# Attention with folded heads: values computed straight from 64-key blocks, second item of a pair shifted into the next step

## The chip, the cores and the metric

The kernel runs on one core of one Trainium2 chip. The metric is device time in microseconds of one execution, lower is better. Engines are named as in the profile: PE (TensorE matmul), PEld (its weight load), DVE (VectorE), ACT (ScalarE), POOL (GpSimd), SP (the queue that issues most DMAs).

## The reference, cut to what matters

Per batch item `x` is 128 tokens of 128 features (B = 32), the context is 77 keys of 128 features. All is float32.

```python
# self-attention, one head over 128 features
Q = x @ Wq.T + bq;  K = x @ Wk.T + bk;  V = x @ Wv.T + bv
x = layernorm(x + softmax(Q @ K.T / 8) @ V @ Wo.T + bo)
# cross-attention, H = 16 heads of 64 over the 77 context keys
q = x @ W_Q[h];  k = ctx @ W_K[h];  v = ctx @ W_V[h]
x = layernorm(x + concat_h(softmax(q @ k.T / 8) @ v) @ W_O)
# 8 experts; each takes the 1024 tokens (of 4096) with its highest gate
G, idx = top_k(softmax(x @ Wr).T, 1024)
x = layernorm(x + scatter_add(G * (gelu(x[idx] @ W1[e] + b1[e]) @ W2[e] + b2[e])))
```

## The kernel before, in words

**Folded weights.** Two set-up products per head are made once: M[h] = W_Q[h] W_K[h]^T / 8 and N[h] = W_V[h] W_O[h]. With them cross-attention needs two context products per head: A[h] = M[h] ctx^T, so that the scores are x1 A[h], and the folded values ctx N[h], so that the output is the sum over heads of probabilities times folded values. Both are made in three float32r products each (high and low halves of weights and context: hi*hi, hi*lo, lo*hi), for four batch items at once: 128 stationary features, 4 x 77 = 308 moving columns. The folded values come out transposed (`VOT`, features on the partitions), and ten 128x128 transposes per batch item turn them into `VO`, which has head-and-key rows on the partitions (16 x 77 = 1232 rows, ten chunks of 128, the last one padded).

**Steps.** Attention goes by pairs of batch items (16 pairs). Step p does cross-attention of pair p ("cross"), self-attention of pair p + 1 ("prep"), and the end of pair p - 1 ("post": its transposed rows and router logits). Steps -2 to 16 exist; the first and last are partial. Steps 1 to 12 are a loop of two steps per turn. In each even step, up to step 12, the values of four items (two pairs) are made (16 "VOT" units); in each odd step the A of four items (16 "A" units). The order inside a step is written out by hand for each engine, and each engine works its list strictly in order: `step` in the TensorE block (L1220), in the ScalarE block (L675), in the VectorE block (L873), in the GpSimd block (L568), in the SP block (L475).

**Hand-over.** TensorE's products go to a ring of four PSUM banks. `UNITS` (L39) lists what uses the ring, in order, and unit k takes bank k mod 4; TensorE waits until the copy of the unit four before has freed the bank. The scores of cross-attention have three banks of their own (`cross_scores`, L1242), and self-attention has one (`small`). Cross-attention of item e (0 or 1): scores, row maxima (L884), subtraction (L889), exp (ACT, L693), row sums (L895), reciprocal (L898), the product with it (POOL, L577), ten transposes (`cross_pT`, L1249), their copies, twenty product records against VO (`cross_out`, L1258), sum with x1 and statistics (L906 to L913), the power -1/2 on POOL (L588), and the normalised rows x2 (L878). Both items of the pair go through all of this in one step. VectorE copies heads 8 to 11 of each set of sixteen (`BY_DVE`), ScalarE the others.

**Self-attention.** Queries and keys are copied with their biases (L731, L733). The row maximum of the scores (L971) times -1/8 (L974) is the bias of the exp, whose scale is 1/8 (L712). The residual `r1` is written to SBUF (L923), its statistics follow (L929 to L936), then the power (POOL, L584) and x1 (L989), which TensorE transposes (L1392) and ScalarE copies (L780). The next step's first scores wait for that copy.

**Start and end.** GpSimd builds constants first, among them a chain of 31 selects (L557). Step -2 makes the values of pairs 0 and 1, then the M half of the set-up. In step 15 nothing is left to overlap, and TensorE runs filler products (`keep_warm`, L1180) between its pieces. Behind the attention stand the top-k by bisection, the gathers, the experts, the scatters and the last layer norm.

## Time and profile before

| | us |
|---|---|
| median of 3 runs | 668.06 (668.0 to 670.12) |
| the profiled execution, its own time | 665.35 |
| its span, first to last instruction | 663.4 |
| PE busy / PEld busy | 555.7 / 464.2 |
| DVE busy / ACT busy / POOL busy | 430.6 / 317.1 / 275.6 |
| mean granted TensorE clock | 0.92 of full speed |

A matmul's busy time includes the pipeline's length, so two neighbours overlap in it. What a product costs in a dense stretch is the distance from its start to the next one's start. In the rows, "x20" is a number of records; a plain float32 product is two records, a float32r product and a transpose are one each.

### The profile page before, as it was taken

To read this page: it belongs to the slowest core of one execution; us is meant where nothing else is said; L and a number is where in the kernel's file an instruction comes from. 1 tells how busy PE (TensorE), PEld (TensorE's weight loads), DVE (VectorE), ACT (ScalarE), POOL (GpSimd) and SP (SyncE) were. 2 spreads that over 40 slices of the span, in tenths; PEclk is the share of its full clock that TensorE was granted. 3 is DMA by queue.
4 is the path that set the end of the run, shared out by engine and by line. 5 is a ranking of instruction groups with operands and counts; after the bars stand their busy time and mean duration, and the time that the engine had idled before them with its cause. 6 is when DMAs were issued, how large, how long until landed. Compare 5 with 4: busy or idle time off the path is not lost.

```text
span 663.4 us, 11726 instructions
## 1 busy us (share of the span) xinstructions
PE 555.7 (84%) x3846; PEld 464.2 (70%) x3846; DVE 430.6 (65%) x1007; ACT 317.1 (48%) x721; POOL 275.6 (42%) x313
## 2 busy tenths in 40 slices
PE   9989999999999999999999979501399999897700
PEld 9868989989988988988988868301277775465600
DVE  3256766766775785685676667588855687424576
ACT  3655855765765675675676632100133334332215
POOL 7203233322322322332232233000677777777756
PEclk9999999999999999999999989655599999979765
DMA  5011220320221122023042100670123355534662
GB/s 187 27 41 39 97 76 14 96 87 10 86 87 51 45 87 89 8 87 96 0 150 72 55 17 9 227 170 0 42 57 109 125 181 176 171 109 142 217 230 111
DMA packets 50547, 61.09 MB, mean 92 GB/s; under 512 B 10578, under 2 KB 36435, under 8 KB 50260
## 3 DMA queue, kind: packets, MB, share of 16 engines
q1 hardware_dynamic: 45984, 52.00, 24.3%
q0 software_dynamic: 4096, 8.66, 4.6%
q8 instruction: 18, 0.29, 0.2%
q14 instruction: 13, 0.11, 0.1%
q10 hardware_dynamic: 436, 0.03, 0.0%
HBM read 35.37 MB, written 25.30 MB: 91 GB/s over the span
## 4 chain that ended last, share of the span: by engine, by line
PE 46%; DVE 25%; issue 12%; POOL 7%; ACT 6%; DMA 3%; DVEq 0%; POOLq 0%; ACTq 0%
PE PS L1238 10%; PE PS L1477 7%; PE PS L1459 7%; PE PS L1264 6%; PE PS L1246 6%; DVE csum L895 3%; POOL spread L612 3%; DVE above L1013 3%; DVE pc L889 3%; PE PS L1255 2%; DVE cmax L884 2%; POOL shared L602 2%; ACT VOeven L673 2%; DMA shared<-table,idx 2%; DVE shared L945 2%
## 5 line engine op out<-in xcount | busy, mean ns | idle before, releaser
L577 POOL TENSOR_TENSOR pn<-pc,crcp 128x1232 f32<-128x1232 f32 x32 | 72.0, 2250 | 180.2 <-DVE crcp L898 180.2
L602 POOL DMA_INDIRECT shared<-table,idx x64 | 63.1, 986 | 66.2 <-DVE idx L1077 47.3
L1238 PE MATMUL PS<-cT_hi,heads_hi 128*128 128x308 f32 x256 | 83.7, 327 | 1.1 <-DVE shared L945 0.6
L673 ACT ACTIVATE shared<-PS 128x308 f32<-128x308 f32 (+1 forms) x144 | 62.1, 472 | 42.2 <-PE PS L1273 29.8
L1238 PE MATMUL PS<-cT_hi,heads_lo 128*128 128x308 f32 x256 | 78.0, 305 | 0.0
L1238 PE MATMUL PS<-cT_lo,heads_hi 128*128 128x308 f32 x256 | 77.5, 303 | 0.0
L1246 PE MATMUL PS<-shared,x1T 128*128 128x512 f32 (+1 forms) x192 | 72.4, 513 | 4.4 <-DVE pc L889 4.0
L612 POOL DMA_INDIRECT spread<-pn,idx x64 | 66.2, 1034 | 19.8 <-issue 17.7
L808 ACT ACTIVATE shared<-PS,b1T 128x512 f32<-128x512 f32 x64 | 44.0, 687 | 56.0 <-PE PS L1459 56.0
L895 DVE TENSOR_REDUCE csum<-pc 128x16 f32<-128x1232 f32 x32 | 45.8, 1430 | 33.6 <-ACT pc L693 33.6
L1477 PEld LDWEIGHTS PS<-w,shared 128*128 128x128 f32 x512 | 63.8, 204 | 4.1 <-issue 3.8
L1477 PE MATMUL PS<-w,shared 128*128 128x128 f32 x512 | 65.0, 288 | 0.1
L1459 PE MATMUL PS<-pT,w 128*128 128x512 f32 x128 | 63.0, 627 | 0.8 <-ACT pT L797 0.7
L673 ACT ACTIVATE pT<-PS 128x512 f32<-128x512 f32 (+1 forms) x96 | 43.5, 527 | 38.5 <-PE PS L1255 38.2
L1246 PEld LDWEIGHTS PS<-shared,x1T 128*128 128x128 f32 x192 | 34.0, 190 | 37.1 <-issue 30.6
L588 POOL TENSOR_TENSOR rs<-ve,mhalf 128x1 f32<-128x1 f32 x32 | 17.3, 541 | 85.9 <-DVE ve L913 85.9
L1238 PEld LDWEIGHTS PS<-cT_hi,heads_hi 128*128 128x128 f32 x256 | 48.4, 189 | 3.3 <-DVE VOT L945 0.8
L673 ACT ACTIVATE VOT<-PS 128x308 f32<-128x308 f32 x96 | 40.2, 435 | 22.0 <-PE PS L1238 22.0
L797 ACT ACTIVATE pT<-PS 128x512 f32<-128x512 f32 x16 | 9.1, 595 | 85.4 <-PE PS L1450 85.4
L1238 PEld LDWEIGHTS PS<-cT_lo,heads_hi 128*128 128x128 f32 x256 | 48.5, 189 | 0.0
L1238 PEld LDWEIGHTS PS<-cT_hi,heads_lo 128*128 128x128 f32 x256 | 48.1, 188 | 0.0
L884 DVE TENSOR_REDUCE cmax<-PS 128x16 f32<-128x1232 f32 x32 | 44.9, 1403 | 3.4 <-PE PS L1246 3.3
(173 smaller groups left out, 1129.1 us busy)
## 6 DMA issues: line engine op xcount, KB each, us to landing
spread<-zeros SPq DMA_DIRECT2D x128, 128.0 KB, 2.1
VOT<-spread SPq DMA_DIRECT2D x64, 256.0 KB, 5.6
xboth<-in_x SPq DMA_DIRECT2D x16, 256.0 KB, 2.7
w<-in_W SPq DMA_DIRECT2D x2, 2048.0 KB, 11.0
table<-x SPq DMA_DIRECT2D x16, 128.0 KB, 1.9
fin<-table SPq DMA_DIRECT2D x1, 2048.0 KB, 20.4
out_x<-fin SPq DMA_DIRECT2D x8, 256.0 KB, 2.0
cin<-in_ctx SPq DMA_DIRECT2D x8, 154.0 KB, 2.6
```

Source lines behind the costliest of these rows:

```text
L577: pool.tensor_tensor(pn[:, e, 0:HK].rearrange("p (h k) -> p h k", h=HEADS), pc[:, e, :].rearrange("p (h k) -> p h k", h=HEADS), crcp[:, e, ...
L602: pool.indirect_dma_start(xg[:, e % 3, h, :], None, table, bass.IndirectOffsetOnAxis(ap=idx[:, e, h:h + 1], axis=0)).then_inc(gathered[e % ...
L612: pool.indirect_dma_start(spread[e], bass.IndirectOffsetOnAxis(ap=idx[:, e, h:h + 1], axis=0), ye[:, e % 2, h, :], None).then_inc(scattere ...
L673: act.activation(dst, src, ACT.Copy).then_inc(free[bank_of(at, name)], 1)
L808: act.activation(hid[:, c, 512 * h:512 * h + 512], PS[:, HID_BANKS[(2 * FC * e + n) % len(HID_BANKS)], :], ACT.Gelu, bias=b1T[:, FC * e + ...
L884: dve.tensor_reduce(cmax[:, e, :], s, AX.X, ALU.max).then_inc(cmax_done, 1)
L895: dve.tensor_reduce(csum[:, e, :], pc[:, e, :].rearrange("p (h k) -> p h k", h=HEADS), AX.X, ALU.add).then_inc(csum_done, 1)
L1238: i = pe.matmul(bank[:, 0:4 * KEYS], w[a][:, h, :], cT[b][:, :], start=(n == 0), stop=(n == 2))
L1246: i = pe.matmul(PS[:, n, 0:b - a], x1T[:, e, :], A[:, 2 * parity + e, a:b], start=True, stop=True)
L1264: i = pe.matmul(bank[:, 0:P], pT[:, e, c * P:(c + 1) * P], VO[parity][:, e, c, :], start=(c == 0), stop=(c == CH - 1))
L1459: pe.matmul(PS[:, HID_BANKS[k % len(HID_BANKS)], :], w1[:, e, c * P:(c + 1) * P], xeT[:, 512 * h:512 * h + 512], start=True, stop=True).th ...
L1477: i = pe.matmul(y_bank(e, h, s), hid[:, c, (4 * h + s) * P:(4 * h + s + 1) * P], w2[:, e, c, :], start=(c == 0), stop=(c == FC - 1))
```

## The change

- The folded values are computed with the keys as the stationary operand, so they come out with keys on the partitions and need no transpose. 64 of the 77 keys of both items of a pair make one stationary block of 128; it is multiplied with four heads at once (512 moving columns). A pair takes four such units ("VO" units, `values`), each of three float32r products. Each unit is copied in two halves of 64 partitions; VectorE copies one unit of the four, ScalarE three.
- The other 13 keys of eight items (104 rows) make a second stationary block: four "rest" units per four pairs, copied to a staging tile, stored to DRAM by 8 DMAs per half and loaded by 2 DMAs per pair into chunks 8 and 9 of VO.
- The normalised probabilities are written on POOL in two instructions, 64 keys and 13 keys of each head, to match the order of rows.
- A is made for eight heads in every step instead of sixteen in every odd one; it is held for three pairs.
- The transposes and the output product of a pair's item 1, with statistics and norm, move to the next step.
- The queries are scaled by -1/8 when they are copied, the row minimum of the scores is the bias of the exp, the multiplication L974 goes, and r1 stays in PSUM.
- The loop has four steps per turn. POOL also copies the high and low halves of the 64 keys (`main_keys`). Step -2 makes the values of pair 0 and the four rest units of the first four pairs. The tile for the returned expert rows moves from VOT to the end of the tile of A.

```diff
-UNITS = [ ... VOT_UNITS ... A_UNITS ... P2T_UNITS ... ]      # two lists, even and odd
+def units_of(phase):
+    units = [(("P2T", 1, g), "post") for g in range(3)]
+    units += [("QK", "prep"), ("V", "prep"), (("AV2", 1), "post")]
+    units += [(("VO", u), "values") for u in range(2)]
+    if phase == 3:
+        units += [(("A", h), "A first") for h in range(8)]
+    heads = [(("A", h), "A even" if phase % 2 == 0 else "A odd") for h in early_heads(phase)]
+    units += heads[0:3] + [(("P2T", 0, g), "cross") for g in range(3)] + [("x2T", "post")]
+    units += heads[3:6] + [(("AV2", 0), "cross")]
+    if phase in (1, 2):
+        units += [(("rest", u), "rest 1" if phase == 1 else "rest 2") for u in range(2 * phase - 2, 2 * phase)]
+    units += heads[6:8] + [(("VO", u), "values") for u in range(2, 4)] + [("LG", "post")]
+    if phase == 2:
+        units += [(("rest", u), "rest first") for u in range(2)]
```

The GpSimd step:

```diff
-                            pn[:, e, 0:HK]..., pc[:, e, :]..., crcp..., ALU.mult).then_inc(pn_done, 1)
+                def main_keys():
+                    if parity == 0:
+                        wait_apart(pool, ct_lo, nth + 2, passed_pool)
+                    for k in range(2):
+                        i = pool.tensor_copy(cmain[k][:, parity, :]..., cT[k]...[:, 2 * parity:2 * parity + 2, 0:KEYS_MAIN])
+                    i.then_inc(cmain_done, 1)
+                def divided(e):
+                    wait(pool, crcp_done, 2 * p + e + 1)
+                    for at_pn, a, b in ((0, 0, KEYS_MAIN), (HEADS * KEYS_MAIN, KEYS_MAIN, KEYS)):
+                        i = pool.tensor_tensor(pn..., pc...[:, :, a:b], crcp..., ALU.mult)
+                    i.then_inc(pn_done, 1)
+                # order: xbo, divided(0), power of item 1 of p - 1, main_keys, power of LN1, divided(1), power of item 0
```

The TensorE step, in its new order (function names as before; `values`, `rest_values` are new):

```diff
+                def values(u):
+                    hi, lo = [t[:, values_pair(at), :] for t in cmain]
+                    h = 8 * (u % 2) + u // 2
+                    n_hi, n_lo = [t[:, h:h + 7:2, :] for t in NN]
+                    done(products(unit(("VO", u)), ((hi, n_hi), (lo, n_hi), (hi, n_lo))), ("VO", u))
-                vo_transposes(...)                  # 20 per pair
                 cross_scores(0)
+                cross_pT(p - 1, 1)                  # if post; 10 filler products first in step 16
                 QK, V
+                cross_out(1, 1 - parity)
                 self_scores()
+                values(0); values(1)                # waits for cmain_done
                 cross_scores(1)
+                heads(mine[0:3])                    # in step -1: heads(range(8)) too, around the self-attention
                 self_transposes()
                 cross_pT(p, 0)
                 x2T
                 self_values()
+                heads(mine[3:6])
                 cross_out(0, parity)
+                rest_values(...)                    # two units in phases 1 and 2, steps 1, 2, 5, 6, 9, 10
+                heads(mine[6:8])
+                values(2)
                 x1T
+                values(3)
                 router()
```

The VectorE step: maximum, subtraction and sum of item 0; cT_lo (even steps), crest_lo; the minimum L971; statistics of (p - 1, item 1); two half copies of VO unit 1; maximum of item 1; norm of (p - 1, item 1); subtraction of item 1; first_norm; sum of item 1; x1; statistics and norm of (p, item 0). In step -1 it copies heads 2, 3, 6, 7 before first_norm and 10, 11, 14, 15 after x1.

```diff
-                                                     r1[:, e, :] (SBUF) in L923, L929, L989; L974 snb = smax * -SELF_SCALE
+                        r1 = small[:, e * P:(e + 1) * P]
+                        i = dve.scalar_tensor_tensor(out=r1, in0=r1, scalar=srcp[:, e:e + 1], in1=xbo[:, e, :], ...)
+                        i = dve.bn_stats(st1[:, e, :], small[:, e * P:(e + 1) * P])
```

The SP step adds `load_rest_keys` (once per turn), `load_rest` (2 DMAs, waiting for the output product of item 1 of the pair before) and `store_rest` (8 DMAs, after two rest units are copied).

## Rows read from the trace of the kernel before

**Rows 1.** Busy time by stage: us, PE, PEld, DVE, ACT, POOL, clock, DMA share, GB/s.
```profile
0.00:41.47 41.47, 37.35 (x288) 35.19 (x288) 14.11 (x45) 22.72 (x53) 18.78 (x63) 1.00 0.25 86
41.47:64.75 23.28, 22.00 (x150) 19.44 (x151) 15.36 (x30) 13.68 (x33) 5.76 (x4) 1.00 0.17 57
64.75:374.86 310.11, 306.08 (x2171) 274.44 (x2169) 213.86 (x448) 198.33 (x490) 92.65 (x91) 1.00 0.21 66
374.86:397.05 22.19, 17.75 (x111) 14.88 (x109) 14.98 (x30) 9.41 (x22) 7.12 (x7) 0.92 0.16 53
397.05:420.20 23.15, 19.21 (x140) 16.20 (x138) 15.29 (x26) 5.91 (x11) 6.12 (x5) 1.00 0.02 6
420.20:663.40 243.20, 153.29 (x994) 104.05 (x994) 157.00 (x429) 67.02 (x112) 145.22 (x143) 0.79 0.45 141
```

**Rows 2.** Who waited for whom, 60 to 400 us: total, times, longest.
```profile
PE PS L1246 <- DVE pc L889: 3.4, 7, 0.5
```

**Rows 3.** Timeline of TensorE: start, us, engine, line, operation, records, idle before.
```profile
160.02 2.23 PE L1246 MATMUL PS<-shared,x1T 128*128 128x512 f32 x6
162.09 1.03 PE L1319 MATMUL PS<-xboth,wT 128*128 128x256 f32 x4
163.40 0.38 PE L1332 MATMUL PS<-ident,x 128*128 128x128 f32 x2
...
192.51 0.30 PE L1238 MATMUL PS<-cT_lo,heads_hi 128*128 128x308 f32 x1
...
196.87 0.31 PE L1238 MATMUL PS<-cT_hi,heads_lo 128*128 128x308 f32 x1
...
201.01 2.39 PE L1264 MATMUL PS<-VOeven,pT 128*128 128x128 f32 x20
203.24 1.25 PE L1255 MATMUL PS<-ident,pn 128*128 128x128 f32 x10
204.33 0.51 PE L1281 MATMUL PS<-wr,x2T 128*128 128x8 f32 x4
```

**Rows 4.** All instructions by line and shape: busy us, mean ns, idle before.
```profile
L838 DVE SCALAR_TENSOR_TENSOR heads_lo<-PS,heads_hi 128x512 fp32r<-128x512 f32 x8 | 5.0, 683 | 8.4 <-ACT heads_hi L661 8.4
L577 POOL TENSOR_TENSOR pn<-pc,crcp 128x1232 f32<-128x1232 f32 x32 | 72.0, 2250 | 180.2 <-DVE crcp L898 180.2
L945 DVE COPY VOT<-PS 128x308 f32<-128x308 f32 x32 | 13.4, 469 | 6.6 <-PE PS L1238 6.6
L961 DVE TENSOR_TENSOR cT_lo<-cin,cT_hi 128x308 fp32r<-128x308 f32 x8 | 3.8, 469 | 0.0
```

**Rows 5.** Timeline of VectorE in step 5, columns as in rows 3.
```profile
162.41 1.43 DVE L884 TENSOR_REDUCE cmax<-PS 128x16 f32<-128x1232 f32 x1
163.87 1.44 DVE L889 TENSOR_TENSOR pc<-PS,cmax 128x1232 f32<-128x1232 f32 x1
...
175.07 1.42 DVE L895 TENSOR_REDUCE csum<-pc 128x16 f32<-128x1232 f32 x1
...
176.69 0.11 DVE L918 RECIPROCAL srcp<-ssum 128x2 f32<-128x2 f32 x1
...
179.95 0.60 DVE L989 TENSOR_SCALAR x<-r,mv,rs 128x128 f32<-128x128 f32 x2 [0.82 <-POOL rs L584]
...
182.25 0.34 DVE L878 TENSOR_SCALAR x<-r,mv,rs 128x128 f32<-128x128 f32 x1 [0.65 <-POOL rs L588]
```

**Rows 6.** Timeline of ScalarE in the same step: the copies of one item's probabilities.
```profile
175.04 1.35 ACT L673 ACTIVATE pT<-PS 128x512 f32<-128x512 f32 x3
```

**Rows 7.** Timeline of TensorE in the first 60 us.
```profile
13.66 0.39 PE L1238 MATMUL PS<-cT_hi,heads_hi 128*128 128x308 f32 x1
```

**Rows 8.** Timeline of POOL at the start: the last of its constants.
```profile
21.64 0.29 POOL L565 CAST before<-beforef 128x128 bf16<-128x128 f32 x1
```

**Rows 9.** Busy time by stage around an idle stretch of TensorE, columns as in rows 1.
```profile
382.00:387.00 5.00, 1.29 (x9) 1.10 (x8) 4.93 (x6) 0.81 (x4) 2.25 (x1) 0.96 0.08 28
387.00:390.00 3.00, 3.00 (x16) 2.96 (x15) 1.67 (x4) 2.81 (x5) 0.00 (x0) 0.50 0.00 0
```

More of the change, by code:

```diff
@@ L49, with runs @@
     while len(units) % RING_BANKS:
         units.append((("none", len(units)), None))
+    return units
+def runs(stage, q):
+    if stage == "prep":
+        return -1 <= q < PAIRS - 1
+    if stage == "cross":
+        return 0 <= q < PAIRS
+    if stage == "post":
+        return 1 <= q <= PAIRS
+    if stage == "ahead":
+        return q % 2 == 0 and -2 <= q < PAIRS - 2
+    if stage == "main keys":
+        return -2 <= q < PAIRS - 2
+    if stage == "A first":
+        return q == -1
+    if stage == "A even":
+        return q % 2 == 0 and 0 <= q < PAIRS - 2
+    if stage == "A odd":
+        return q % 2 == 1 and -1 <= q < PAIRS - 2
+    if stage == "values":
+        return q == -2 or 0 <= q < PAIRS - 1
+    if stage == "rest first":
+        return q == -2
+    if stage == "rest 1":
+        return q % PHASES == 1 and 1 <= q < PAIRS - 4
+    if stage == "rest 2":
+        return q % PHASES == 2 and -2 <= q < PAIRS - 4
+    return False
@@ new lines, in step @@
+                if values:
+                    values_copy(0)
+                    values_copy(1)
+                if prep:
+                    self_exp()
+                if first == -1:
+                    self_pT()
+                    heads_copy(range(8))
+                if heads:
+                    heads_copy(mine[0:3])
+                if prep and cross:
+                    self_pT()
+                if cross:
+                    if first == 0:
+                        act.wait_ge(rest_out, 16 * 4 * PHASES)
+                    cross_pT(0)
@@ L957, in step @@
                     cross_sub(0)
-                if even:
+                    cross_sum(0)
+                if runs("ahead", first):
                     wait(dve, ct_hi, nth + 2)
@@ L1347, in step @@
-                if even:
-                    wait(pe, ct_lo, nth + 2)
-                if isinstance(p, int) and p == -2:
-                    for k in range(FIRST):
-                        setup_wait_copied(pe, k)
-                if isinstance(p, int) and p == -1:
-                    for k in range(FIRST, len(SETUP)):
-                        setup_wait_copied(pe, k)
-                if products:
-                    heads(0, 4)
-                if first:
-                    self_values()
@@ L1389, in step @@
+                if runs("rest 1", first):
+                    wait(pe, cr_lo, turn + 2)
+                    rest_values(0)
+                    rest_values(1)
+                if runs("rest 2", first):
+                    if first == -2:
+                        pe.wait_ge(cr_lo, 1)
+                    rest_values(2)
+                    rest_values(3)
+                if ahead:
+                    heads(mine[6:8])
+                if runs("values", first):
+                    values(2)
                 if prep:
@@ L1393, in step @@
                     i.then_inc(self_full, 1)
-                if cross:
-                    cross_out(1)
+                if runs("values", first):
+                    values(3)
+                if post:
+                    router()
+                if runs("rest first", first):
+                    rest_values(0)
+                    rest_values(1)
+                if first == -2:
+                    for k in range(FIRST, len(SETUP)):
+                        set_up_unit(k)
+                    pe.wait_ge(route_in, 16 * 3)
             attention_steps(pe, step)
             for k in range(RING_BANKS):
-                n = sum(active(q, stage) for q in range(-2, PAIRS + 1) for j, (_, stage) in enumerate(UNITS[q % 2])
+                n = sum(runs(stage, q) for q in range(-2, PAIRS + 1) for j, (_, stage) in enumerate(UNITS[q % PHASES])
                         if j % RING_BANKS == k)
```

600 lines of the change are left out of this document (340 added, 260 removed).

## The prediction

> **What bounds the kernel now.** I read the busy shares by stage first [rows 1]. Steps 1 to 13 of the attention last 310.11 us, 23.85 us a step; TensorE is busy in 306.08 of them at full clock, VectorE in 213.86, ScalarE in 198.33. The start takes 41.47 us, step 0 23.28, step 14 22.19, and step 15 up to the last x2 23.15. The last 243.2 us are top-k and experts, which the change leaves alone. Then the waits: the largest of TensorE's own inside the steps is 3.4 us in 7 waits [rows 2]. So it is TensorE's list of work that sets the length of a step. Overlapping busy times don't price it, so I take distances between starts [rows 3]: three float32 score products (6 records, 1232 columns) 162.09 - 160.02 = 2.07 us; QK and V 1.31; a float32r product of 308 columns (196.87 - 192.51) / 31 = 0.141; an output product (20 records) 2.23, so 4 records are 0.45; ten transposes 1.09; the router 0.4 (its four records show 0.51).
>
> **TensorE's work in a step, before and after.** Both: scores 2 x 2.07, probability transposes 2 x 1.09, outputs 2 x 2.23, QK and V 1.31, self scores and values 2 x 0.45, three double transposes 3 x 0.22, router 0.37: 14.0 us. Before there are also 24 products of 308 columns on average for A and 24 for the values, 48 x 0.141 = 6.77, and 20 value transposes, 2.18: 22.97 us, against 23.85 measured, so 0.9 a step are stalls and refills. After: 24 products for A, 3.38; 12 products of 512 columns. The trace has no float32r product that wide. Bounds: 512 columns in proportion to 0.141 are 0.234; 0.141 plus the additional 204 columns at the rate of the score products (two records per column, 2.07 / 2464 = 0.84 ns a record column, a half of it if float32r goes once) is 0.227; nothing above 308 columns free of charge is the floor, 0.141. I take 0.22, near the upper two: 2.64. Sum 20.05 us. In six of the thirteen steps (1, 2, 5, 6, 9, 10) two rest units add 6 x 0.22 = 1.32. Thirteen steps: 13 x 20.05 + 7.9 = 268.6 us without a stall, 280 if the old 0.9 stays in each.
>
> **Does another engine bind then?** Time from the start of a step's first scores; VectorE's list with distances of [rows 5]. Maximum of item 0 at 2.4, subtraction 3.85 to 5.3. ScalarE has by then copied the three groups of the older item's probabilities (1.35 each time [rows 6]) and QKV, and the exp runs 5.35 to 6.6. Sum and reciprocal (1.62) to 8.3. Minimum 0.4; statistics of the older item 1.1 (179.95 + 0.6 to 182.25 - 0.65) to 9.8; the two half copies to 11.0; maximum 12.4; norm 12.7; subtraction 14.0; first_norm 2.3 to 16.3; sum 18.0; x1 18.6. TensorE comes to x1's transposes at 18.8, so it is just not kept waiting. They, VO unit 3 and the router end at 20.05, and the next scores start. The probabilities of item 0 leave POOL at 10.9, TensorE wants them at 12.0; the older item's rows x2 are ready at 12.7, wanted at 13.1; bank 2 (output of item 0, freed by VectorE behind x1 at 18.8) is wanted at 19.0. In even steps cT_lo pushes VectorE's list by 0.35 and TensorE waits some 0.2. Everything fits, with 0.2 to 1 us of room: I put 0.4 a step on it, 5.2 in all. So 273.8 against 310.1: **-36.3**.
>
> **Single edits.** Half copies: the nearest row is a 512-column pass from PSUM, 0.683 [rows 4]; two are 1.25, below nothing is excluded as the four head copies (4 x 0.4) that they replace are gone; cover VectorE's list above. If 64 partitions cost double, the list grows by 1.2. POOL's product in two instructions: 2.25 for one now; two cost between 2.25 and 4.5; I take 2.5, since 1232 elements are the same and one more start is added. Cover: 1.1 us before TensorE wants them; behind it on POOL stand the power that the norm at 12.3 waits for, so the upper end would cost 1.2 on VectorE's list. L974's removal saves 0.4 of VectorE's list, counted. Negated scaling rides on a copy that exists: nothing. ScalarE: eight head copies, six half copies, a rest copy per two steps in place of twelve heads and six VO copies: about 17 us of 20.5, no bound. POOL's main_keys: two copies of 128 elements, under 1 us between item 0's product (10.9) and LN1's power (16.3). SP: load_rest waits for an output product done at 6.7, then 8 clears, then the store of x2; store_rest last; the loaded rows are wanted 28 us after their issue. Nothing on the path; if SP were late it would show at `cross_out(0)`.
>
> r1 in PSUM: two statistics passes and two scalings now read PSUM. The row of a copy from PSUM, 308 elements in 469 ns, is as long as an SBUF-only subtraction of the same size, 469 [rows 4]; so I charge nothing for it. The Trainium skill (VectorE: DVE Perf Modes, "The TRN2 errata" and "Why PSUM operands drop a tier") puts 62 cycles more on a PSUM source and takes the doubled rate from a float32 scaling. By that rule the four instructions would add an estimated 0.4 us to VectorE's list and use up the room; the pair of rows speaks against the fixed part of it.
>
> **Start: a loss.** The first value products ran at 13.66 [rows 7]. Now they wait for POOL's main_keys, and POOL is in its chain of constants until 21.93 [rows 8]; two memsets less (0.35), two copies more: 22.3. TensorE then has 8 units of 3 x 0.22, 5.3 us. It has idled 8 us, though, and rows show what follows: after 5 us with 1.29 of busy time, 387 to 390 ran at clock 0.50, which is 1.2 GHz, and the next stretch was back near full [rows 9]. That costs 1.7. Fold and M set-up 3.7 us as before: step -1 starts at 33, 8 us later than before. In step -1 the value transposes go (3.3 us), but heads 14 and 15 wait for VectorE's copies of 10 and 11, which stand behind x1: about 14.6 us instead of 16.4. First scores at 47.5: **+6.1**. **Step 0** has no older item: VectorE's list is shorter by the statistics and norm, and x1 ends it: 18.6 against 23.3, **-4.7**. **Step 14** has no heads; VectorE's list holds it at 19.9 against 22.2: **-2.3**.
>
> **End: a loss.** In step 15 the older item's transposes and output stand in front of the filler and the second scores, which start at 9.4 instead of 5.7. The rest of the chain follows: maximum 11.8, subtraction 15.0, exp 16.5, sum 18.2, POOL's product 20.7, transposes 22.3, copies 23.3, output 25.6, statistics, power and norm 2.3: 27.9 against 23.1: **+4.8**. The tail behind is unchanged.
>
> Sum: -36.3 + 6.1 - 4.7 - 2.3 + 4.8 = -32.4. The profiled execution took 665.35 (span 663.4 and 1.95 around it), 2.7 below the median of the runs; 668.06 - 32.4 = 635.7, **636 us**.
>
> **Rivals.**
> 1. *VectorE's list becomes the bound.* For: it has 0.2 us of room, and four of its neighbours are priced from rows of other shapes. Against: its sum of work is 16 us. With POOL's pair at its upper end (+1.2) and 0.5 for reads of PSUM and half copies, x1 ends at 20.3 and a step lasts 21.6, with a rest unit 22.3. 7 x 21.6 + 6 x 22.3 = 285, 11 more than forecast, and steps 0 and 14 1.7 each: 650 us.
> 2. *Slower: wide float32r products run at half rate.* Mechanism: a product of 512 columns takes 0.43 us, as a record of the float32 scores does (2.07 / 2464 x 512). Place: all 16 x 12 value and 48 rest products, 240 x 0.21 = 50 us: 686 us. It turns the sign from 0.355 us per product. Against: the 308-column products go once, at 0.141.
> 3. *The stalls stay.* What kept TensorE waiting 0.9 us a step before was the order of hand-overs; if it stays, 280 instead of 273.8: 642 us.
>
> **How the numbers follow.** Forecast 0.45, stalls stay 0.25, VectorE's list 0.22, half rate 0.05, and 0.03 for a change that moves nothing because gains are eaten. The range goes from the stall-free sum with 0.21 per product and a start 2 us shorter (628) to the second case with 2 us more (652). Within 0.3% is what a measurement here can't tell from no change. Faster 0.92 (the first three), same 0.03, slower 0.05.
>
> **What would show it.** Right: first scores near 47 us with TensorE idle from 14 to 22; distances of 20.1 to 21.5 us between steps; products of 512 columns 0.22 us apart; step 15 some 5 us longer. Wrong: TensorE waiting for x1 (L989) or x2 in every step (rival 1); products 0.4 apart (rival 2); waits for `rest_in` ahead of the outputs, which I charged nothing.

## The result, and the profile after

| | before | changed |
|---|---|---|
| median of the runs, us | 668.03 (666.09 to 670.12, 4 runs) | 635.27 (634.73 to 635.82, 4 runs) |
| ratio | | 0.951, 95% interval 0.948 to 0.954 |
| profiled execution, its time and its span | 665.35, 663.4 | 635.82, 633.9 |
| PE busy / PEld busy | 555.7 / 464.2 | 524.8 / 423.6 |
| DVE / ACT / POOL busy | 430.6 / 317.1 / 275.6 | 415.4 / 316.8 / 289.0 |

The median is 32.8 us lower and lies where it was forecast. The profiled executions differ by 29.5 us only, because that of before was 2.7 below its median and that of the changed kernel 0.5 above its own. The forecast of -32.4 was made between profiled executions, so measured like for like it is 3 us too large.

The busy shares by stage of the changed kernel, cut where the first cross scores of steps 0, 1, 14 and 15 and the last norm begin; the last cut of [rows 1] lies 0.4 us later, where that norm ends (start:end, length, busy us and count of PE, PEld, DVE, ACT and POOL, then granted clock, DMA share, GB/s):

```profile
0.00:50.76 50.76, 36.34 (x234) 31.80 (x234) 15.45 (x47) 18.63 (x40) 19.38 (x65) 0.89 0.31 92
50.76:70.80 20.04, 18.60 (x98) 14.25 (x99) 13.97 (x26) 10.71 (x26) 5.64 (x7) 0.93 0.24 79
70.80:342.96 272.16, 271.89 (x1779) 235.52 (x1779) 198.66 (x413) 199.12 (x450) 104.31 (x146) 1.00 0.31 92
342.96:362.20 19.24, 17.64 (x112) 14.13 (x112) 14.78 (x31) 11.86 (x26) 6.01 (x7) 1.00 0.39 128
362.20:390.20 28.00, 24.43 (x190) 21.80 (x189) 14.81 (x26) 9.38 (x19) 7.65 (x10) 1.00 0.02 6
390.20:633.90 243.70, 155.92 (x994) 106.13 (x994) 157.71 (x430) 67.16 (x112) 146.01 (x143) 0.78 0.45 141
```

The third line holds the gain: thirteen steps in 272.16 us instead of 310.11, with TensorE busy in all but 0.27 us. Seven steps without rest units last 20.3 us (one 20.8), six with them 21.6. The first line holds a loss: the first scores begin at 50.76 instead of 41.47. That start shows in TensorE's timeline (start, length, engine, line, operation, count, and in brackets the idle time before and what ended it):

```profile
22.22 0.77 PE L1408 MATMUL PS<-heads_hi,cmain_hi 128*128 128x512 f32 x1 [7.57 <-POOL cmain_lo L700]
...
26.70 0.73 PE L1408 MATMUL PS<-heads_hi,crest_hi 128*104 128x512 f32 x1 [1.57 <-DVE VOeven L1117]
...
29.35 0.62 PE L1408 MATMUL PS<-heads_hi,cmain_hi 128*128 128x512 f32 x1
29.78 0.42 PE L1408 MATMUL PS<-heads_hi,cmain_lo 128*128 128x512 f32 x1
30.04 0.40 PE L1408 MATMUL PS<-heads_lo,cmain_hi 128*128 128x512 f32 x1
...
48.96 0.41 PE L1408 MATMUL PS<-cT_hi,heads_hi 128*128 128x308 f32 x1 [1.65 <-DVE shared L1106]
...
50.76 3.79 PE L1438 MATMUL PS<-shared,x1T 128*128 128x512 f32 x6 [0.47 <-ACT x1T L857]
```

After 7.57 us without work TensorE runs at the lower of its two clocks, 1.2 GHz (granted clock 0.50): the value products are 0.43 us apart until 29.78, then 0.26, and 0.23 after that. From 29.78 to 49 the granted clock is 1.00. Then it falls a second time: the first scores take 3.79 us where those of the next steps take 2.3, at 0.50.

In a full step, the product of 512 columns shows its price in the same view:

```profile
142.28 0.40 PE L1408 MATMUL PS<-heads_hi,cmain_hi 128*128 128x512 f32 x1
142.51 0.39 PE L1408 MATMUL PS<-heads_hi,cmain_lo 128*128 128x512 f32 x1
142.74 0.39 PE L1408 MATMUL PS<-heads_lo,cmain_hi 128*128 128x512 f32 x1
142.97 1.45 PE L1438 MATMUL PS<-shared,x1T 128*128 128x512 f32 x3
```

From 142.28 to 142.97 are three products, 0.23 us each. VectorE's and POOL's timelines of the step that begins at 134.35, around the parts that changed:

```profile
144.30 1.39 DVE L1117 COPY shared<-PS 64x512 f32<-64x512 f32 x2
145.72 1.44 DVE L1050 TENSOR_REDUCE cmax<-PS 128x16 f32<-128x1232 f32 x1
...
149.61 0.49 DVE L1094 BATCH_NORM_STATS2 st<-PS 128x6 f32<-128x128 f32 x2
...
152.25 0.64 DVE L1166 TENSOR_SCALAR x<-PS,mv,rs 128x128 f32<-128x128 f32 x2
```

```profile
142.73 2.52 POOL L708 TENSOR_TENSOR pn<-pc,crcp 128x1024 f32<-128x1024 f32 x2 [7.22 <-DVE crcp L1064]
...
152.41 2.43 POOL L708 TENSOR_TENSOR pn<-pc,crcp 128x1024 f32<-128x1024 f32 x2 [0.92 <-DVE crcp L1064]
```

The first of these two fences holds three of the prediction's prices: two half copies 1.39 to 1.42 us (predicted 1.25), statistics from PSUM 0.49 for two, and x1 done at 152.25 + 0.64 = 152.9, which is 18.5 us after the scores (predicted 18.6). The last line of it and the last of POOL's overlap; that becomes important below.

### The profile page after: what moved, and what is told of

Same layout as the page of the kernel before. It is cut to its first block, busy times and chain, and to the rows that moved or that the text cites. A ratio compares the mean times of both kernels' runs of the same rounds, so it can differ in the third digit from the quotient of the medians.

```text
span 633.9 us, 10905 instructions
## 1 busy us (share of the span) xinstructions
PE 524.8 (83%) x3402; PEld 423.6 (67%) x3402; DVE 415.4 (66%) x971; ACT 316.8 (50%) x670; POOL 289.0 (46%) x375
## 4 chain that ended last, share of the span: by engine, by line
PE 68%; DVE 13%; POOL 9%; issue 4%; DMA 3%; ACT 2%; POOLq 0%; ACTq 0%; DVEq 0%
PE PS L1408 17%; PE PS L1438 11%; PE PS L1460 10%; PE PS L1655 7%; PE PS L1673 7%; PE PS L1448 5%; POOL spread L753 3%; DVE above L1188 3%; POOL shared L743 2%; PE PS L1510 2%; POOL groupf L674 2%; DMA shared<-table,idx 2%; DVE pc L1245 1%; PE PS L1476 1%; PE PS L1489 1%
## 5 line engine op out<-in xcount | busy, mean ns | idle before, releaser
L708 POOL TENSOR_TENSOR pn<-pc,crcp 128x1024 f32<-128x1024 f32 x64 | 78.6, 1248 | 146.6 <-DVE crcp L1064 146.6
L971 ACT ACTIVATE shared<-PS,b1T 128x512 f32<-128x512 f32 x64 | 44.0, 687 | 58.4 <-PE PS L1655 58.4
L814 ACT ACTIVATE shared<-PS 128x308 f32<-128x308 f32 x120 | 47.5, 434 | 30.3 <-PE PS L1408 30.2
L814 ACT ACTIVATE pT<-PS 128x512 f32<-128x512 f32 (+2 forms) x100 | 45.8, 528 | 22.5 <-PE PS L1448 18.4
L1055 DVE TENSOR_TENSOR pc<-PS,cmax 128x1232 f32<-128x1232 f32 x32 | 46.0, 1438 | 0.6
L726 POOL TENSOR_TENSOR rs<-ve,mhalf 128x2 f32<-128x2 f32 x16 | 11.2, 702 | 76.7 <-DVE ve L1101 76.7
L1655 PEld LDWEIGHTS PS<-pT,w 128*128 128x128 f32 x128 | 21.3, 196 | 36.0 <-ACT shared L971 23.9
L1408 PE MATMUL PS<-cT_hi,heads_hi 128*128 128x308 f32 x128 | 43.0, 336 | 2.3 <-DVE shared L1106 1.7
L826 ACT ACTIVATE pc<-pc 128x1232 f32<-128x1232 f32 x32 | 39.7, 1241 | 2.8 <-DVE pc L1055 2.8
L1448 PE MATMUL PS<-ident,pn 128*128 128x128 f32 (+1 forms) x320 | 40.2, 273 | 0.5 <-POOL pn L708 0.5
L842 ACT ACTIVATE VOeven<-PS 64x512 f32<-64x512 f32 x48 | 28.4, 592 | 24.1 <-PE PS L1408 23.4
```

The source lines that it names most:

```text
L708: i = pool.tensor_tensor(pn[:, e, at_pn:at_pn + HEADS * (b - a)].rearrange("p (h k) -> p h k", h=HEADS), pc[:, e, :].rearrange("p (h k) -> ...
L814: act.activation(dst, src, ACT.Copy).then_inc(free[bank_of(at, name)], 1)
L1055: dve.tensor_tensor(pc[:, e, :].rearrange("p (h k) -> p h k", h=HEADS), s, cmax[:, e, :].unsqueeze(2).to_broadcast([P, HEADS, KEYS]), ALU. ...
L1408: i = pe.matmul(bank, a, b, start=(n == 0), stop=(n == len(pairs) - 1))
L1448: i = pe.transpose(bank[0:rows, (c - a) * P:(c - a + 1) * P], pn[:, e, n:n + rows], ident[:, :])
L1655: pe.matmul(PS[:, HID_BANKS[k % len(HID_BANKS)], :], w1[:, e, c * P:(c + 1) * P], xeT[:, 512 * h:512 * h + 512], start=True, stop=True).th ...
```

## The experiments

Twelve kernels ran, in three sets of four. In the first and third set the kernel before had medians of 667.9 and 666.7 us. The second set ran on a chip on which it had 709.65. In its kernels the part behind the attention took some 285 us at clock 0.74 instead of 243 at 0.78, while steps 1 to 13, where an edit leaves them alone, took 272.16 and 272.15 us as in the changed kernel. Absolute times are therefore not compared across sets, only ratios and lengths of stages; the changed kernel itself was not run in the second and third set.

**The changed kernel again**, as the base of the first set.

> The changed kernel again, as the control of the kernels beside it. Same as its first timing: 635.3 us (634.7 to 635.8).

Measured: 634.92 us (632.74 to 635.76), ratio 0.950, interval 0.947 to 0.954; first scores 49.69, steps 1 to 13 in 272.17 us. The start varies between executions, the steps do not. Here the wait for the keys is as long, but TensorE was back at full clock after the gap in the middle of the value products, which are 0.23 to 0.29 us apart from this line on:

```profile
26.79 0.45 PE L1408 MATMUL PS<-heads_hi,crest_hi 128*104 128x512 f32 x1 [1.57 <-DVE VOeven L1117]
```

That alone makes the first scores 1.07 us earlier than in the first profile. The start's other part that varies is the second fall of the clock. Of the kernels below with this start and its waits, the one with the scalings ahead of the reciprocal has it at the first scores as well (3.79 us), the one without fillers in step 15 has it earlier, in the heads' products, and those with the small product alone and with two value units on VectorE have none (first scores in 2.34 us). Where it comes it costs 1.5 us. What decides it is open, so these 1.5 us are not put down to an edit.

### The start

**POOL makes the keys of step -2 in the middle of its constants.**

```diff
                 pool.wait_ge(consts, 18 + n + P // E)
+                if n == 0:
+                    pool.wait_ge(ct_lo, 1)
+                    for k in range(2):      # the two casts of main_keys()
+                        i = pool.tensor_copy(cmain[k][...], cT[k][...])
+                    i.then_inc(cmain_done, 1)
...
-                if runs("main keys", first):
+                if runs("main keys", first) and first != -2:
                     main_keys()
```

> POOL copies the 64 keys of step -2 after 16 of its 31 constant selects instead of behind all of them. Theory A (the wait at the start is the cause of the loss there, and the half clock follows from it): TensorE starts the value products at about 13.9 instead of 22.2 and at full clock, so 8.3 + 3.7 = 12 us come back; first scores at 39, 623.5 us. Theory B (something else at the start is late too, the weights of M or the copies of the rest units): less than half of it, 629 us or more.

Measured: 623.7 us (620.86 to 624.78), ratio 0.934, interval 0.932 to 0.937, against 0.950 in the same set. POOL's and TensorE's timelines of this kernel:

```profile
3.57 8.53 POOL L674 TENSOR_SCALAR_AFFINE_SELECT groupf<-groupf 128x128 f32<-128x128 f32 x16
12.17 0.29 POOL L680 CAST cmain_hi<-cT_hi 128x128 fp32r<-128x128 f32 x1
12.41 0.29 POOL L680 CAST cmain_lo<-cT_lo 128x128 fp32r<-128x128 f32 x1
12.65 7.98 POOL L674 TENSOR_SCALAR_AFFINE_SELECT groupf<-groupf 128x128 f32<-128x128 f32 x15
```

```profile
13.66 0.48 PE L1415 MATMUL PS<-heads_hi,cmain_hi 128*128 128x512 f32 x1
...
16.87 0.45 PE L1415 MATMUL PS<-heads_hi,crest_hi 128*104 128x512 f32 x1 [1.57 <-DVE VOeven L1124]
```

The value products start at 13.66, as they did before the change [rows 7], and at full clock. First scores are at 39.75, 9.9 us earlier than in the base of this set, and step 0 takes 18.58 us, the 18.6 that was predicted for it. Theory A holds: two casts of 0.29 us that stood at the end of a chain of constants cost 11.2 us (634.92 - 623.7). The traces divide it: 8.7 us of waiting (22.32 - 13.66), 1.3 in the value products at half clock, and 1.5 in step 0, where the clock did not fall (that part may not be the keys' doing, as said above).

**The wait kept, the clock held up.** 34 filler products ahead of the wait for the keys.

```diff
                 if runs("values", first):
+                    if first == -2:
+                        keep_warm(34, 6)
                     wait(pe, cmain_done, ...)
```

> The wait for POOL stays, but TensorE runs 34 filler matmuls in it (about 7.6 us), so it does not stand idle. Theory A (7.4 us of value products at half clock are the result of the idle stretch): the clock stays at full speed, the eight units take 5.5 us instead of 9.2, 631.5 to 632.5 us. Theory B (the clock plays no part, the copies of the units set their rate): no change, 635.3.

Measured: 632.4 us (630.84 to 633.96), ratio 0.946, interval 0.943 to 0.950, which overlaps the base's. The trace is clearer than the times: the eight units end at 29.92 instead of 31.43 in the base of this set, yet the first scores begin at 49.69 in both. Two stretches of this kernel and then the two of the base that answer to them (columns as in the stages above) show what took it back:

```profile
36.00:38.00 2.00, 0.55 (x5) 0.39 (x5) 0.42 (x1) 0.81 (x4) 0.00 (x0) 1.00 0.64 121
38.00:42.00 4.00, 4.00 (x19) 4.00 (x20) 0.96 (x2) 1.25 (x4) 0.00 (x0) 0.57 0.74 198
```

```profile
37.50:39.50 2.00, 0.55 (x5) 0.39 (x5) 0.42 (x1) 0.81 (x4) 0.00 (x0) 1.00 0.67 124
39.50:43.00 3.50, 3.50 (x26) 3.50 (x27) 1.06 (x3) 2.10 (x5) 0.00 (x0) 1.00 0.72 184
```

Here the clock fell behind the first exp of the self-attention, and the heads' products ran slower for 4 us; then step 0 takes 18.55 us instead of 20.08. The base lost the same 1.5 us at its first scores, so that fall only changed its place: step 1 begins at 68.24 instead of 69.77, and those 1.5 us are what the value products gained. Theory A holds for them. The medians differ by 2.5 (634.92 - 632.4), but their intervals overlap. The missing keys cost the larger part.

**Heads 10, 11, 14 and 15 of the first step copied by ScalarE.**

```diff
-            return at.first == -1 and h % 8 in FIRST_HEADS_BY_DVE
+            return at.first == -1 and h in FIRST_HEADS_BY_DVE
```

> In the first step that makes heads for a pair, four of the head banks (10, 11, 14 and 15) are copied out by ScalarE instead of VectorE. TensorE had waited 1.65 us for VectorE's copies of 10 and 11, which stand behind the first x1. Theory A (that wait sets the first cross scores at 50.76, and the half clock that follows it makes those scores 3.79 instead of 2.23 us): first scores 1.3 to 1.7 us earlier, step 0 up to 1.5 us shorter, 632 to 634 us. Theory B (ScalarE's copies delay x1's transposed copy, on which the same scores wait, by their own four times 0.6 us): first scores at the same place or up to 1 us later, 635 to 636 us.

Measured (second set): 676.41 us (675.27 to 678.4), ratio 0.954, interval 0.951 to 0.956. First scores 48.94, step 0 18.57: step 1 starts at 67.51, against 69.77 to 71.63 in the four kernels that have the changed kernel's start and step 0 (with r1 in SBUF in one of them). From the set-up's product L1373, where the value products are done, to the first scores are 16.57 us (32.37 to 48.94) instead of 18.26 in both executions of the changed kernel: the wait of 1.65 us is gone and nothing took its place. So the first half of theory A holds, with 1.7 us, and theory B falls. The second half, that the wait brings the half clock of the first scores, isn't shown: three kernels with the wait have those scores at full clock too. The ratio of the whole doesn't show the gain.

### The shift of the half pair

**Item 1's transposes, output, statistics and norm back in their own step**, the keys stationary and the self-attention as changed.

```diff
-    units = [(("P2T", 1, g), "post") for g in range(3)]
-    units += [("QK", "prep"), ("V", "prep"), (("AV2", 1), "post")]
+    units = [("QK", "prep"), ("V", "prep")]
...
-    units += heads[6:8] + [(("VO", u), "values") for u in range(2, 4)] + [("LG", "post")]
+    units += heads[6:8] + [(("P2T", 1, g), "cross") for g in range(3)]
+    units += [(("VO", u), "values") for u in range(2, 4)] + [(("AV2", 1), "cross"), ("LG", "post")]
```

with the engines' lists moved in the same way.

> Item 1's transposes, output, statistics stay in their own step, as before; everything else of the change is kept. Theory A (without the shift the chain through VectorE and POOL to item 1's product, ready 19.4 us into the step, is the bound and the output product has to follow it): a step lasts about 24.7 us, 13 x 24.7 = 321 instead of 272, step 0 four more, step 15 five less: 683 us. Theory B (TensorE's list is the bound either way and the shift is worth only the stalls of 0.9 us a step that the kernel before had): 647 us.

Measured: 696.98 us (696.39 to 699.29), ratio 1.043, interval 1.040 to 1.046: slower than the kernel before. Step 1 begins at 76.08 and step 14 at 398.09, 24.8 us a step against 20.9, with TensorE busy in 286.84 of 322.01 us. TensorE's largest group of waits in this kernel from 76 to 400 us (waiting and waited for, us in total, times, longest), and one case of it in its timeline:

```profile
PE PS L1447 <- POOL pn L709: 25.8, 26, 2.0
```

```profile
168.90 1.62 PE L1447 MATMUL PS<-ident,pn 128*128 128x128 f32 x10 [1.96 <-POOL pn L709]
171.59 0.63 PE L1575 MATMUL PS<-ident,x 128*128 128x128 f32 x2
```

The shorter list of TensorE is worth nothing in this order without the shift: TensorE has run out of other work before item 1's probabilities leave POOL, it waits for them in 26 places, and the transposes that follow at 171.59 take 0.63 us instead of 0.44. The chain of theory A holds, and its 24.7 us a step. The shift removes no instruction, and yet the keys' 2.9 us less of TensorE's work a step (22.97 to 20.05 in the prediction's sum) count only with it. Two things stay open: the kernel before had no shift either and took 23.85 us a step, and what makes this one 0.9 longer was not isolated; and the shift with the old values was not run.

### The self-attention's part

**The whole part undone**: queries unscaled, the maximum times -1/8 on VectorE, r1 in SBUF.

```diff
-                                      ALU.min).then_inc(smin_done, 1)
+                                      ALU.max).then_inc(smin_done, 1)
+                    dve.tensor_scalar(snb[:, :], smin[:, :], -SELF_SCALE, None, ALU.mult).then_inc(snb_done, 1)
...
-                        i = dve.scalar_tensor_tensor(out=r1, in0=r1,
+                        i = dve.scalar_tensor_tensor(out=r1s[:, e, :], in0=r1,
```

> The self-attention part of the change undone, everything else kept: the queries unscaled, the scale again in the exponential with an extra small VectorE product on the maxima, and the residual written to SBUF instead of back into PSUM. It adds one VectorE instruction of about 0.1 us and its wait to each step. Theory A (TensorE's list sets the step, with 271.89 of 272.16 us busy in steps 1 to 13, and what PSUM costs VectorE against SBUF is nothing, as the statistics took 0.49 us for two from either): the step keeps its length, the whole is 0 to +2 us on the changed kernel's 635 us. Theory B (the small product with its hop to ScalarE delays the exponential, and with it the probabilities and x1, by 0.3 to 0.5 us a step that TensorE then waits): +4 to +7 us over 15 steps.

Measured (second set): 722.47 us (720.4 to 723.91), ratio 1.018, interval 1.015 to 1.020. Both theories fail. Steps 1 to 13 take 307.87 us (75.70 to 383.57) instead of 272.16: 2.75 a step, and the whole gain of the change is gone with an edit that the prediction priced at 0.4 us of VectorE's list for the product and at nothing for r1. Two groups of VectorE's instructions in this kernel, from 95 to 300 us (line, operation, shapes, count, busy, mean ns of one, idle before):

```profile
L1171 DVE TENSOR_SCALAR x<-r,mv,rs 128x128 f32<-128x128 f32 x18 | 19.5, 1125 | 0.0
L1143 DVE TENSOR_SCALAR snb<-smin 128x2 f32<-128x2 f32 x9 | 13.6, 1516 | 0.3
```

A product of two elements per partition takes 1516 ns. The next three kernels ask why.

**r1 in SBUF alone.** Of the diff above the last two lines, and the statistics and the scaling reading `r1s`.

> The changed kernel with the self-attention's residual in SBUF alone undone; the scaling stays in the queries. With the whole self-attention part undone a step took 22.85 us instead of 20.27, and two rows had grown: the two scalings to x1 took 2.17 us together instead of 0.64, and the small product on the maxima 1.71 us. Both stood beside POOL's pair of products on the probabilities. Theory A (a VectorE scaling whose operands are all in SBUF is held up until a running POOL product ends; from PSUM it is not): the two scalings take 1.5 to 2.2 us, a step 1.1 to 1.5 us longer, 21.4 to 21.8 us without rest units, and the whole 15 to 20 us more than the changed kernel's. Theory B (the scalings were late only because the small product was): the scalings take 0.6 to 0.7 us and the step stays at 20.3.

Measured: 656.63 us (652.42 to 658.32), ratio 0.983, interval 0.978 to 0.987. Steps 1 to 13 take 287.14 us, 1.15 a step more. VectorE's and POOL's timelines of this kernel:

```profile
158.31 0.25 DVE L1065 RECIPROCAL crcp<-csum 128x16 f32<-128x16 f32 x1
158.48 2.16 DVE L1167 TENSOR_SCALAR x<-r,mv,rs 128x128 f32<-128x128 f32 x2
```

```profile
158.64 2.42 POOL L709 TENSOR_TENSOR pn<-pc,crcp 128x1024 f32<-128x1024 f32 x2 [0.92 <-DVE crcp L1065]
```

**The small product alone.** Of the diff above the first three lines, r1 in PSUM.

> The changed kernel with the scaling back in the exponential, which needs the small product of 128x2 elements on VectorE again; the residual stays in PSUM. Theory A (as for the residual: all its operands are in SBUF and it starts just behind the start of POOL's product of item 0, so it lasts until the first of POOL's two instructions or both have ended): the product takes 1.4 to 1.7 us instead of the 0.1 to 0.2 that two elements need, a step 1.0 to 1.5 us longer, the whole 13 to 20 us more. Together with the residual's 1.1 to 1.5 that makes the 2.6 us of the whole part. Theory B (the product's own length is 0.2 us and the hand-over to ScalarE costs 0.3): a step is 0 to 0.3 us longer.

Measured: 654.72 us (652.27 to 656.01), ratio 0.982, interval 0.979 to 0.985. Steps 1 to 13 take 289.86 us, 1.36 a step more. The same two views of this kernel:

```profile
145.91 1.43 DVE L1142 TENSOR_SCALAR snb<-smin 128x2 f32<-128x2 f32 x1
...
156.27 0.64 DVE L1170 TENSOR_SCALAR x<-PS,mv,rs 128x128 f32<-128x128 f32 x2
```

```profile
145.29 2.53 POOL L710 TENSOR_TENSOR pn<-pc,crcp 128x1024 f32<-128x1024 f32 x2 [6.74 <-DVE crcp L1066]
...
156.43 2.43 POOL L710 TENSOR_TENSOR pn<-pc,crcp 128x1024 f32<-128x1024 f32 x2 [0.92 <-DVE crcp L1066]
```

POOL's record holds two instructions: the first takes 2.02 us at 145.29 and 1.92 at 158.64, the second 0.55. The small product ends at 147.34, when the first of them does (145.29 + 2.02 = 147.31). At 38.3, in step -1, where POOL stands still from 34.5 to 45.6, the same instruction of this kernel takes 0.17 us. The scalings with r1 in SBUF end at 160.64, again with the first (158.64 + 1.92 = 160.56); of the two, one takes 0.25 us and the other 2.0. With r1 in PSUM the same scalings beside the same product take 0.64 us together.

**r1 in SBUF, but the scalings ahead of the reciprocal** that lets POOL's product start.

```diff
                     dve.tensor_reduce(csum[:, e, :], ...).then_inc(csum_done, 1)
+
+                def cross_rcp(e):      # cross_rcp(0) stays behind the sum of item 0
                     wait(dve, csum_done, 2 * p + e + 1)
                     dve.reciprocal(crcp[:, e, :], csum[:, e, :]).then_inc(crcp_done, 1)
...
                         dve.tensor_scalar(x1[1 - parity][:, e, :], r1s[:, e, :], ...)
                 if cross:
+                    cross_rcp(1)
                     second_stats(p, 0, parity)
```

> The residual in SBUF as before the change (scaling still in the queries), and on VectorE the two scalings to x1 moved ahead of the reciprocal of item 1's sum, so that POOL's product of item 1, which waits for that reciprocal, cannot have started. Same instructions, same operands, another order of two. Theory A (the scalings are held up by POOL's running product): they take 0.6 to 0.7 us again, x1 is as early as in the changed kernel or 0.2 us earlier, the step is back at 20.3 us (21.6 with rest units), and the whole within 0.5% of the changed kernel. Theory B (operands in SBUF are slow by themselves, or another engine's traffic slows them): 1.1 us each as with the whole part undone, a step of 21.4 us or more.

Measured: 635.5 us (633.89 to 636.85), ratio 0.953, interval 0.949 to 0.956, that of the changed kernel; steps 1 to 13 take 271.91 us (changed 272.16). VectorE and POOL:

```profile
152.43 0.59 DVE L1170 TENSOR_SCALAR x<-r,mv,rs 128x128 f32<-128x128 f32 x2
152.94 0.24 DVE L1067 RECIPROCAL crcp<-csum 128x16 f32<-128x16 f32 x1
```

```profile
153.26 2.43 POOL L709 TENSOR_TENSOR pn<-pc,crcp 128x1024 f32<-128x1024 f32 x2 [1.30 <-DVE crcp L1067]
```

Same instructions and operands, other order, 21 us less than with r1 in SBUF and the order as it was, 15.2 of them in steps 1 to 13. Theory A holds. So it is neither SBUF as such nor the scaling: a VectorE scaling from SBUF to SBUF that meets a running POOL product waits until that ends. The Trainium skill states this (SBUF — State Buffer, "Who interferes with whom"): VectorE's two-port modes and GpSimd share one pair of ports, and the one that comes second "fully blocks". This case's traces agree, with 1.43 to 2.16 us, and a source in PSUM kept VectorE out of it.

### The room on VectorE, and the end

**VectorE copies two value units of four.**

```diff
-VALUES_BY_DVE = (1,)
+VALUES_BY_DVE = (0, 1)
```

> VectorE also copies the first of the four value units of a step, which ScalarE copied: about 1.4 us more on VectorE's list in each of 16 steps and about 1.2 us less on ScalarE's. This measures the room on VectorE's list beside TensorE's. Theory A (VectorE's list from the scores to the x1 that the next scores need has less than 0.5 us of room, as the walk of the changed kernel has it: x1 ends 18.5 us after the scores in a step of 20.3): the added copy delays x1 and the step grows by 0.9 to 1.1 us, 647 to 651 us on the whole, with TensorE idle that much in each step. Theory B (VectorE's idle time of some 5 us a step takes the copy up, since the copy stands before a wait for TensorE): the step grows by under 0.2 us, the whole by under 3 us.

Measured (second set): 694.85 us (691.4 to 697.73), ratio 0.979, interval 0.975 to 0.982. Steps 1 to 13 take 287.84 us, 1.21 more a step for 1.4 added. That is theory A, a little above its 0.9 to 1.1: VectorE's list has about 0.2 us of room (1.4 less 1.21) beside TensorE's.

**No fillers ahead of step 15's second scores and of step 16's transposes.**

```diff
-                    keep_warm(10 if first == PAIRS else 0)
+                    keep_warm(0)
...
-                    keep_warm(14 if alone else 0)
+                    keep_warm(0)
```

> Leaves out the 14 filler products ahead of step 15's second half pair's scores and the 10 ahead of the transposes after it, which the changed kernel has because steps 15 and 16 have no next pair to prepare. Theory A (they stand in front of work that is ready before they end, so the path shortens by what they cover): the second scores began at 371.93 behind fillers that ran to about 371.9, and the last stretch from 362.20 to 390.20 gets 1 to 3 us shorter, 632 to 634 us on the whole. Theory B (the fillers keep the granted clock at full speed; without them it falls to half, and the scores, transposes and outputs of the end, some 3.4 us of work at full clock, take twice that): 0 to +3 us, with half clock in the slices from 368 to 390.

Measured (second set): 678.43 us (674.18 to 680.66), ratio 0.954, interval 0.951 to 0.958. The second scores come 6.60 us after the first instead of 9.73, but from step 15's first scores to the last norm are 27.28 us instead of 27.92. TensorE in this kernel:

```profile
369.62 2.23 PE L1438 MATMUL PS<-shared,x1T 128*128 128x512 f32 x6
...
381.77 1.31 PE L1448 MATMUL PS<-ident,pn 128*128 128x128 f32 x10 [1.56 <-POOL pn L708]
383.97 4.61 PE L1460 MATMUL PS<-shared,pT 128*128 128x128 f32 x20 [0.89 <-ACT pT L814]
```

Both theories are half right. The 14 fillers stood in the way; the 10 kept the clock up (without them 0.50 was granted from 384 to 389). Without them the last output product takes 4.61 us instead of 2.47 and hands back most of the gain.

**Together**: the early keys, the heads by ScalarE, the 14 fillers out, the 10 kept.

> Three edits on the changed kernel that gained alone, together: POOL makes the keys of step -2 in the middle of its chain of constants, ScalarE instead of VectorE copies heads 10, 11, 14 and 15 of the first step, and the 14 fillers ahead of step 15's second scores are gone, while the 10 ahead of the transposes of step 16 stay, since without them the granted clock fell to half at 384 and the last output product took 4.61 instead of 2.47 us. Theory A (they add up, as each lies on another stretch of the path): first scores 39.7 less 0.5 to 1.5 us, step 15 to the last x2 26.0 instead of 28.0, together -13 to -15 us on the changed kernel, a ratio to the kernel before of 0.928 to 0.933 where the changed kernel had 0.951. Theory B (the heads' copies gained only because TensorE's clock was down at the start, which the earlier keys already mend): -12.5 to -13.5, ratio 0.931 to 0.935.

Measured: 619.11 us (618.8 to 620.96), ratio 0.928, interval 0.926 to 0.931, the fastest kernel here, and within theory A's ratio. Step 15 to the last norm takes 25.68 us, 2.2 less. But the first scores are at 40.70, 0.95 later than with the early keys alone, as ScalarE's timeline shows:

```profile
36.82 3.38 ACT L821 ACTIVATE shared<-PS 128x308 f32<-128x308 f32 x8 [1.29 <-PE PS L1415]
40.26 0.38 ACT L864 ACTIVATE x1T<-PS 128x256 f32<-128x256 f32 x1
```

x1's transposed copy stands behind eight head copies; with VectorE copying four of the heads it began at 39.32. So the heads' edit should be left out once the keys are early; that combination wasn't run. In the traces this kernel reaches the last norm 1.3 us before the one with early keys alone (376.33 and 377.61), and the two profiled executions are equally long (620.96 and 620.86); the rest of the difference between their ratios, 0.928 and 0.934, is seen in no stage of the attention.

## Why the prediction was right, and where not

Term by term, in us between the same marks (the last norm ends at 420.16 before and at 390.46 after):

| | predicted | measured |
|---|---|---|
| first scores later | +6.1 | +9.3 |
| step 0 | -4.7 | -3.2 |
| steps 1 to 13 | -36.3 | -38.0 |
| step 14 | -2.3 | -3.0 |
| step 15 to the end of the last norm | +4.8 | +5.1 |
| the rest | 0 | +0.2 |
| span | -32.4 | -29.5 |

- **The bound was read rightly.** TensorE's list set the step [rows 1 to 3], and the sum of that list priced it: 20.05 us without a stall against 20.27 measured. The 0.4 us a step put on for stalls was too much. The wide products, the one unknown with far ends, cost 0.23, near the two upper bounds, so rival 2 falls. The pair of POOL's products cost 2.43 to 2.52 us, predicted 2.5.
- **"The stalls stay" falls.** The 0.9 us a step of before went with the shift. Without the shift a step is 4 us longer than with it; the prediction had no term for that.
- **Rival 1 was nearer than its 0.22 says.** The changed kernel has 0.2 us of room on VectorE, and it has them because r1 lies in PSUM and the small product is gone.
- **"r1 in PSUM ... I charge nothing for it"** is right for what it asked, two statistics at 0.49 us, as from SBUF before (the row at 177.57 below), and two scalings at 0.64 against 0.60 [rows 5]. The four instructions cost 0.04 us more than from SBUF, not the 0.4 of the prediction's other estimate. It asked the wrong question. It compared the instruction by itself, not beside the neighbour that it gets in the new order, where the edit saves 1.15 us a step.
- **"L974's removal saves 0.4"** was too small for the same reason: in the new order it would cost 1.5 us on VectorE's list and 1.36 a step. The trace of before had the clue. There, VectorE and POOL show:

```profile
171.56 0.70 DVE L974 TENSOR_SCALAR snb<-smax 128x2 f32<-128x2 f32 x1
...
177.57 0.49 DVE L929 BATCH_NORM_STATS2 st<-r 128x6 f32<-128x128 f32 x2
...
178.49 0.64 DVE L936 TENSOR_SCALAR ve<-mv 128x2 f32<-128x2 f32 x1
```

```profile
169.98 2.25 POOL L577 TENSOR_TENSOR pn<-pc,crcp 128x1232 f32<-128x1232 f32 x1 [7.17 <-DVE crcp L898]
176.86 2.25 POOL L577 TENSOR_TENSOR pn<-pc,crcp 128x1232 f32<-128x1232 f32 x1 [4.62 <-DVE crcp L898]
```

The two small products, the first and the last of VectorE's rows, end with POOL's product: 172.26 and 172.23, 179.13 and 179.11. Their lengths were taken for their own. In step -1 of the same trace, at 28.4, where POOL stood still, L974 took 0.17 us instead of 0.70.
- **The start: the mechanism was right, the size off.** 22.3 was predicted for the first value product and 22.22 came; 3.7 for fold and set-up and 3.70 came; 14.6 for step -1 and 14.56 came. The miss of 3.2 us lies in the eight value units. "8 units of 3 x 0.22, 5.3 us" is the term that failed most: at full clock, in the kernel with early keys, they take 7.85 us (13.66 to 21.51), because TensorE waits 1.57 us for VectorE's copy of a value unit and shorter times for others, which the prediction didn't have. "That costs 1.7", for the half clock, came out at 2.4 here (10.28 us from 22.22 to 32.50) and at 1.3 in the changed kernel's second execution, so its size was about right. The 1.4 us by which step 0 missed are the second fall of the clock, which the prediction didn't have; where its first scores run at full clock, step 0 takes the predicted 18.6 (18.58 with early keys, 18.58 without the fillers of step 15).
- **The end** was walked wait by wait and came out at 5.1 us, predicted 4.8.
- **The range's lower end** doesn't add up: 635.7 less 5.2 for the stalls, 2.4 for 0.01 us on 240 products and 2 for the start is 626, where 628 stands. Nothing hangs on it.

That the median was met owes something to the two profiled executions lying on different sides of their medians; steps 1 to 14 came out 2.3 us better and the start with step 0 4.7 us worse, so part of the agreement is errors that cancel.

## What to carry to other kernels

Price an instruction beside the neighbour that it will have on the other engines, not from its mean. A tiny VectorE instruction of over half a microsecond that ends when a POOL instruction ends, as in the four cases here, is waiting for it; the same line at a place where POOL stands still gives its own length. Give it a PSUM operand, or move it ahead of what starts POOL. When an engine's list gets shorter, ask whether its inputs come early enough to use it; and look for the new first input of an engine at the end of another engine's set-up.

## What the runs showed of the hardware that was not expected

- A VectorE scaling of 128x2 elements from SBUF to SBUF took 1516 ns on average beside a POOL product of some 2.0 us, and 168 ns where POOL stood still; one of 128x128 up to 2.0 us instead of 0.3 (two in 0.59). The same scaling with its source in PSUM took 361 ns beside the same POOL product. VectorE's copies from PSUM at 144.30, beside POOL's product from 142.73 to 145.25, kept their length.
- A float32r product of 512 columns costs 0.229 us, one of 308 columns 0.141: 0.43 ns for each further column. At half clock the former costs 0.43 us.
- After 7.57 us of idling TensorE's clock stayed at the lower level for 7.6 us of work with one gap of 1.57 us in it. After 8.12 us of idling, in the changed kernel's second execution, the first six products (22.32 to 25.2) ran at it and those behind the gap, from 26.79, at the full one.
- Copies of 64 partitions are no cheaper than copies of 128: 512 columns from PSUM took 688 ns on VectorE and 592 on ScalarE, where copies over 128 partitions of the same width took 594 on ScalarE (`pT`) and a pass of another kind took 683 on VectorE [rows 4].
